# A fused macaron layer with a 64-state scan: the loop over inner batches written out, with constant waits

## What is computed

```
def step(state, inp):
    x_t, dt_t, B_t, C_t = inp
    dA = jnp.exp(dt_t[:, :, None] * A[None])
    state = state * dA + (dt_t * x_t)[:, :, None] * B_t[:, None, :]
    y_t = jnp.einsum('bds,bs->bd', state, C_t)
    return (state, y_t)
...
y = y + x_ssm * D[None, None, :]
y = y * jax.nn.silu(z)
return x + y @ Wout
```

## Time and profile before

| | us |
|---|---|
| median of 3 runs | 5524.71 |
| lowest, highest | 5524.02, 5534.78 |
| the profiled execution: time | 5548.79 |
| the profiled execution: span from first to last instruction | 5546.0 |

### The profile page before, as it was taken

How to read it: one execution, slowest core, us unless ns; L and a number is a source line. 1 busy time by engine, 2 the same in 40 slices (tenths; PEclk the granted TensorE clock), 3 DMA queues, 4 the chain that set the end, 5 groups by cost and what they waited for, 6 DMA issues and landing times.

```text
span 5546.0 us, 203591 instructions
## 1 busy us (share of the span) xinstructions
PE 4869.8 (88%) x85070; PEld 3076.2 (55%) x85070; DVE 4916.4 (89%) x4595; ACT 3918.0 (71%) x6659; POOL 5028.8 (91%) x2310
## 2 busy tenths in 40 slices
PE   4798989989899898988989899898988989899887
PEld 2455555555555555555555555555555555555554
DVE  1699999989998998989989999998989989999997
ACT  3777777767777676776767778676776767766564
POOL 0699998999989899898999989999898999999997
PEclk9899999999999999999999999999999999999999
DMA  5565655656556565565656556565565655556553
GB/s 166 151 168 196 166 185 177 176 186 162 191 168 183 180 172 186 165 186 175 171 193 165 184 179 176 192 162 193 171 182 183 170 189 170 182 184 172 190 179 123
DMA packets 579015, 977.63 MB, mean 176 GB/s; under 512 B 294881, under 2 KB 328450, under 8 KB 510466
## 3 DMA queue, kind: packets, MB, share of 16 engines
q1 hardware_dynamic: 313858, 961.82, 54.2%
q10 hardware_dynamic: 264192, 2.11, 2.8%
HBM read 875.74 MB, written 88.08 MB: 174 GB/s over the span
## 4 chain that ended last, share of the span: by engine, by line
POOL 59%; issue 25%; PE 8%; DMA 3%; DVE 2%; ACT 1%; POOLq 1%; ACTq 0%; DVEq 0%; SPq 0%
POOL H L665 56%; PE pUB L729 3%; PE Y L755 3%; DMA Cb<-scratch_c 2%; DVE H L607 2%; PE pP L686 1%; POOL lnv L641 1%; POOL dto L646 1%; PE pP L692 1%; POOL duo L652 1%; POOLq L664 0%; PE pA L775 0%; DVE cv L558 0%; PE pA L769 0%; ACT junk L193 0%
## 5 line engine op out<-in xcount | busy, mean ns | idle before, releaser
L665 POOL TENSOR_TENSOR H<-H,Cb 128x1024 f32<-128x1024 f32 x2048 | 4796.1, 2397 | 322.0 <-DVE H L607 315.3
L607 DVE TENSOR_TENSOR_SCAN H<-dA,pUB 128x512 f32<-128x512 f32 x4096 | 4675.8, 1202 | 444.0 <-PE pUB L729 417.7
L444 ACT ACTIVATE dA<-DT,w_negA 128x512 f32<-128x512 f32 x4096 | 2620.4, 711 | 1271.2 <-DVE H L607 1267.8
L729 PEld LDWEIGHTS pUB<-Bd,UT 64*64 64x64 f32 x65536 | 1961.7, 134 | 1357.7 <-issue 1339.0
L729 PE MATMUL pUB<-Bd,UT 64*64 64x128 f32 x65536 | 2267.3, 274 | 452.5 <-DVE H L607 380.0
L755 PE MATMUL Y<-H,w_ident 64*64 64x512 f32 x16384 | 2034.1, 602 | 103.8 <-POOL H L665 99.8
L755 PEld LDWEIGHTS Y<-H,w_ident 64*64 64x64 f32 x16384 | 681.6, 135 | 680.9 <-issue 664.5
L686 PE MATMUL pP<-hT,w_Win 128*128 128x512 f32 x512 | 281.1, 675 | 15.3 <-DVE cv L558 12.1
L692 PE MATMUL pP<-U,w_dt_w 128*128 128x512 f32 x512 | 257.3, 627 | 6.6 <-DVE ev L621 4.8
L444 ACT ACT_TABLE_LOAD x178 | 228.4, 1283 | 3.3
L558 DVE SCALAR_TENSOR_TENSOR cv<-pP,w_conv_w,cv 128x511 f32<-128x511 f32 (+2 forms) x192 | 139.3, 725 | 34.0 <-ACT cv L382 33.7
(11 more groups left out here) (80 smaller groups left out, 1740.4 us busy)
## 6 DMA issues: line engine op xcount, KB each, us to landing
Cb<-scratch_c SPq DMA_DIRECT2D x512, 1024.0 KB, 5.3
Bd<-scratch_diag SPq DMA_DIRECT2D x512, 512.0 KB, 4.2
scratch_diag<-H SPq DMA_DIRECT2D x16, 1024.0 KB, 18.0
scratch_z<-zo SPq DMA_DIRECT2D x64, 256.0 KB, 5.7
scratch_dt<-dto SPq DMA_DIRECT2D x64, 256.0 KB, 7.3
scratch_ut<-uto SPq DMA_DIRECT2D x64, 256.0 KB, 6.2
DT<-scratch_dt SPq DMA_DIRECT2D x64, 256.0 KB, 5.1
UT<-scratch_ut SPq DMA_DIRECT2D x64, 256.0 KB, 5.9
```

Of the source, the lines that this page charges most:

```text
L444: last = nc.scalar.activation(dA[:, n % DAR, j, :], DT[:, k, :], ACT.Exp, scale=c["negA"][:, k, GS * blk + j:GS * blk + j + 1])
L607: last = nc.vector.tensor_tensor_scan(H[:, n % HR, 2 * i + j, :], dA[:, n % DAR, 2 * i + j, :], pUB[:, i, :].rearrange("p (t s) -> p s t", ...
L665: nc.gpsimd.tensor_tensor(h[:, j:j + 2, :], h[:, j:j + 2, :], Cb[:, blk % 2, j:j + 2, :], ALU.mult).then_inc(times_c, 1)
L729: last = nc.tensor.matmul(out, UT[rows, k, j * P + h * HP:j * P + h * HP + HP], Bd[rows, blk % 2, i, j * P:(j + 1) * P].rearrange("p (t s) ...
```

## The change

The loop is written out: steps 1 to 13 are traced one after the other in Python, so there is no jump back and every count is a constant. The instruction `pe.sem_inc(pe_go, 1)` goes at its four places, so the wait (the last one, where there are several) stands at the first product. Two table entries move the fourth turn of `duo` from unit 50 to 52 on PE, its copy on ACT from 52 to 54 and its store on SP from 53 to 56. The loads of `DT` and `UT` move from units 60 and 61 to 50 and 54 (tiles 0 and 1 of the next step) and from units 4 and 5 to 10 and 14 (tiles 2 and 3).

```diff
-SPS = {"load x": (0,), "load r": (2,), "store z": (6, 10, 14, 18), "store C": (22,), "store dt": (31, 37, 43, 49),
-       "store u": (37, 43, 49, 53), "load z": (28, 29, 36, 37), "store out": (48,), "store r": (42,)}
+SPS = {"load x": (0,), "load 2": (10, 14), "load 0": (50, 54), "load r": (2,), "store z": (6, 10, 14, 18), "store C": (22,), "store dt": (31, 37, 43, 49),
+       "store u": (37, 43, 49, 56), "load z": (28, 29, 36, 37), "store out": (48,), "store r": (42,)}
...
-        "store B": (25, 26, 29, 30, 31, 32, 35, 37), "dt": (27, 33, 39, 45), "log": (28, 34, 40, 46), "turn u": (36, 42, 48, 52),
+        "store B": (25, 26, 29, 30, 31, 32, 35, 37), "dt": (27, 33, 39, 45), "log": (28, 34, 40, 46), "turn u": (36, 42, 48, 54),
...
-       "turn u": (34, 40, 46, 50), "turn 1": (13, 16), "turn c": (32, 35), "turn 3": (51, 54)}
+       "turn u": (34, 40, 46, 52), "turn 1": (13, 16), "turn c": (32, 35), "turn 3": (51, 54)}
...
         step(0, True, False, True, True)
-        with engine.Fori(1, NB - 2) as b:
+        for b in range(1, NB - 2):
             step(b, True, True, True, True)
...
-                    if scan and n in (4, 5):
-                        load_du(b, n - 2)
+                    if scan and n in when["load 2"]:
+                        load_du(b, 2 + when["load 2"].index(n))
...
-                    if proj and n in (GN - 4, GN - 3):
-                        load_du(q, n - GN + 4)
+                    if proj and n in when["load 0"]:
+                        load_du(q, when["load 0"].index(n))
...
                 pe.wait_ge(state_done, at(2 * u + i - 1))
-                pe.sem_inc(pe_go, 1)
                 for j in range(NJ):
```

More of the change, by code:

```diff
@@ L261, in layers @@
     d_in, c_in = [sem(f"d_in{i}") for i in range(2)], [sem(f"c_in{i}") for i in range(2)]
-    u_kept, pe_go, d_blank, d_st, rs_one = sem("u_kept"), sem("pe_go"), sem("d_blank"), sem("d_st"), sem("rs_one")
+    u_kept, d_blank, d_st, rs_one = sem("u_kept"), sem("d_blank"), sem("d_st"), sem("rs_one")
     decay, forced, state_done, times_c, summed, skip, gated = (sem(n) for n in ("decay", "forced", "state_done", "times_c", "summed", "skip", "gated"))
@@ L271, in ffns @@
     def ffns(b):
-        return min(b + 2, NB) if isinstance(b, int) else b + 2
+        return min(b + 2, NB)
     def steps(engine, step):
@@ L325, in step @@
                 c_, q, a = b - 1, b + 1, b + 2
[L326 to L329, removed]
+                when = SPS
                 for n in range(GN):
@@ L337, in step @@
                     if scan and n % 2 == 0 and seq < 2 * NBLK - 1:
-                        load_block(b if n < HALF else twin, seq + 1, GN * b + n)
-                    if scan and n in (4, 5):
-                        load_du(b, n - 2)
+                        load_block(b, seq + 1, GN * b + n)
+                    if scan and n in when["load 2"]:
+                        load_du(b, 2 + when["load 2"].index(n))
                     if close and n in when["load r"]:
@@ L370, in step @@
                         load_block(q, 0, GN * q - 2)
-            again = sp.alloc_register("again")
             sp.wait_ge(zero, at(1))
@@ L419, in store_diagonals @@
                 act.wait_ge(b_out, at(q + 1))
-                if isinstance(q, int) and q < 2:
+                if q < 2:
                     act.wait_ge(d_blank, at(16 * FILLS * (q + 1)))
```

## The result

The kernel after takes 5455.3 us (median of 4 runs, 5452.2 to 5459.0). The kernel before, run beside it on the same chip, takes 5529.7 us (median of 4, 5524.0 to 5537.1). The ratio is 0.985 with a 95% interval of 0.9834 to 0.9866; the two medians differ by 74.5 us, and their quotient, 0.9865, lies at the upper edge of that interval. The time lies inside the predicted range, 8 us above the predicted 5447. The profiled execution took 5459.0 us where the one before took 5548.8, and the sum made against that time had said 5459.

What follows compares the result with a forecast made beforehand. POOL, busy about 314 us a step, was taken as the bound, with only its idle time winnable. Against the profiled 5548.8 us: -87.2 -8 -2 +7, about -90, 5459; for the runs 5447 us, range 5420 to 5485.

Steps and rivals of the forecast that it cites:

- The jumps, -87.2: Loop written out: removing twelve jumps back per engine wins the surplus of steps 2 to 13 over step 1, 87.2 us.
- The direct part, 5.6 us a jump: At a jump: PE's 3.82 us pause reaches POOL as 4.5 us, about 5.6 with the slow products behind.
- The waits at the products, -8: PE's waits at products: each real wait 0.10 us shorter, five a step count, 16 scanned steps: 8 us.
- upper bound of 34: PE's waits at products: if all 21 waits of a step counted, 2.1 us a step, 34 us in all.
- The fourth turn, -2: Turn of duo near unit 51: moving it can win POOL's next gap, 0.23 us; 0 to 3.5 us, taken as 2.
- DT and UT, 0: Loads on SP: moving them gains nothing at the boundary, and Cb's slack covers the new place; 0 us.
- No Cb wait: Profile after: expected to show no wait for a Cb transfer.
- More code, 0: Instruction fetch: written-out code is read no more than before, as the looped body was fetched anew every turn; 0 us.
- Rival (c): Written-out code stalls on its own fetch, 1.57 us each; at seven a step slower, 5590 us; chance 0.04.
- Slow stretches that come back, +7: Clock at 1.2 GHz: slow stretches return in two of thirteen steps, 3.1 us each, rounded up to 7 us.
- Rival (a): Jumps go but all thirteen steps have slow-clock stretches, 3.1 us each, 40 us instead of 7; 5480 us; chance 0.13.
- two readings of the 24 us: Profiled run's 24.1 us excess: in the stalls that go, runs end at 5459 us; elsewhere, at 5435; middle taken.

Runs made afterwards that it cites:

- The first experiment: Kernel before with only the loop changed: steps 1 to 13 written out, counts constant, separate wait instructions, turns and loads unmoved; 5469.7 us, ratio 0.9875.
- the wait apart: Kernel after with the separate wait instruction put back on PE at its four places; 5475.8 us, beside 5458.3 for the kernel after on the same chip.
- the last experiment: Kernel after with first sums into X, first feed-forward's products and two norm 2 statistics moved later; 5495.5 us, beside 5460.9 for the kernel after.
- second set: Kernel after unchanged, run again beside its versions with the separate wait, turn or loads put back; 5458.3 us, ratio 0.9858 to the kernel before.
- third set: Kernel after unchanged, run on another chip beside a repeat of its version with the loads back; 5460.9 us, ratio 0.9837 to the kernel before.
- first set: Kernel after unchanged, the runs of the main result; 5455.3 us beside 5529.7 for the kernel before, ratio 0.9850.

## Why the prediction held, point by point

**The bound.** POOL is still the pace, busy for 314 us of each step. Its idle time in a plain step is 13.6 us, as "near 14" had said; step 1 of before was a good picture of what every step would become.

**The jumps, -87.2.** Right in cause, 18 us too large as a term. The loop alone brought 69 us (interval 58 to 80). The prediction took the whole surplus of steps 2 to 13 over step 1 as the jumps' and set 7 us of clock against it; the split is 68 us of jumps and 19 us of slow stretches. The first experiment kept 3959.3 - 12 x 328.4 = 18 us over step 1, of which some 7 are its two stalls and the rest its five slow steps. The direct part, 5.6 us a jump, was close: 68 / 12 = 5.7, and five jumps in place of twelve follow it. What the step left out is that the sum has two engines in it: with PE's jump gone, DVE's 1.03 us comes to the surface. One row was misread: of the 13 waits of PE for "issue" in steps 2 to 13 of before, ten are at jumps and not twelve. The pauses at the jumps into steps 10 and 11, 3.02 and 3.12 us, stand under DVE's name, and the three others are 0.25, 0.80 and 1.57 us inside steps.

**The waits at the products, -8.** The latency was right, and what it is worth was not. Over the waits for the scan in steps 2 to 13, `force` starts 0.05 us behind it in the median in after, and 0.15 us behind it with the wait apart. The scan ahead of a waiting `force` in after:

```profile
1915.05 1.21 DVE L603 TENSOR_TENSOR_SCAN H<-dA,pUB 128x512 f32<-128x512 f32 x1
...
1916.31 1.10 PE L724 MATMUL pUB<-Bd,UT 64*64 64x128 f32 x32 [0.16 <-DVE H L603]
```

It ends at 1916.26 and the product starts at 1916.31, 0.05 us later, where it was 0.15. It reaches POOL at four places a step before unit 51, not five, for 0.3 us and not 0.5, and the undisturbed step is no shorter for it (327.7 us with and without). Yet the whole edit brought 14 to 17 us, by fewer stalls of straight code and, in these runs, fewer slow steps. Neither had a term, and neither is shown to follow from the shorter wait. The prediction's upper bound of 34 held the amount, but by luck: it had been worked out from the latency alone.

**The fourth turn, -2.** Nothing. The gap of 0.23 us that it was to remove is gone in plain steps with the turn at either place.

**DT and UT, 0.** Right. POOL waited for one Cb of step 0 in after, 1.6 us, and for one in the same step of before, 1.9 us. In the later steps of each profiled run at most one Cb was late: by 0.6 us in three of the six runs with the loads at the new place, and by 0.3 to 1.6 us in five of the eight at the old.

```profile
POOL H L661 <- DMA Cb<-scratch_c: 1.6, 1, 1.6
```

"No Cb wait" was thus not quite what was seen, and the row of before had been there to read.

**More code, 0.** Right, and a little better: the instruction queues of after carry less than the earlier trace rows.

```profile
q8 instruction: 668, 10.94, 0.8%
q14 instruction: 142, 1.16, 0.1%
```

Together 12.1 MB against 13.7. Rival (c), stalls of straight code, stayed rare but was larger where it came than its price of 1.57 us: 3.6 and 4.9 us in the first experiment, 3.9 and 3.9 in the kernel with the wait apart, and none that the waits list for `force` over steps 2 to 13 of the kernel after. Step 0 of after has two, 1.33 and 1.23 us. The change got by with so few because the waits stand at the products, or by chance; that isn't shown.

**Slow stretches that come back, +7.** Right in size for the kernel after. Its six profiled runs (three as it is, three with the turn or the loads back) have 18 slow steps among 72, each 3.0 us longer than a plain one: 12 x 0.25 x 3.0 = 9 us. Rival (a), all steps slow, is what the last experiment became by another edit: 331.2 us a step, 35 us lost where (a) had put 33. So it was a real rival.

**From the profile to the runs.** The sum against the profiled time, -90, came out as 89.8. It held because errors cancelled. In the spans, the loop alone goes from 5546.0 to 5472.2, that is 73.8 less where the sum had -87.2 + 7 = -80; the other three edits go on to 5457.0, that is 15.2 less where it had -10. The prediction had two readings of the 24 us by which that run lay over the others, and took the middle. The first was the better: in after the profiled run lies 4 us over its median, and the time is 5455 and not 5435. So the excess probably sat in what went; no trace of a shorter run of before is there to show it.

## What stays open

Two steps of one run can be alike to the hundredth of a microsecond and still part at the clock. In the kernel after (second set), step 3 and then step 6, PE:

```profile
1254.52 1.10 PE L724 MATMUL pUB<-Bd,UT 64*64 64x128 f32 x32 [1.86 <-DVE H L603]
1255.55 3.32 PE L682 MATMUL pP<-hT,w_Win 128*128 128x512 f32 x4
...
2240.69 1.10 PE L724 MATMUL pUB<-Bd,UT 64*64 64x128 f32 x32 [1.86 <-DVE H L603]
2241.72 1.98 PE L682 MATMUL pP<-hT,w_Win 128*128 128x512 f32 x4
```

Both come 81 us after POOL's first product of their step, behind the same wait of 1.86 us. The same four products take 3.32 us in one and 1.98 in the other, and the granted clock of the 4 us around them is 0.57 and 1.00:

```profile
1255.50:1259.50 4.00, 4.00 (x26) 1.67 (x24) 3.31 (x3) 3.42 (x8) 4.00 (x3) 0.57 0.13 49
2241.70:2245.70 4.00, 4.00 (x52) 2.06 (x52) 4.00 (x4) 3.41 (x8) 3.88 (x3) 1.00 0.31 114
```

The work ahead of them doesn't tell them apart, nor does the DMA rate of 49 against 114 GB/s, since the other plain steps of this run have 49 to 64 at the same place. What differs is when the step begins, seen against the clock record. Within one run, the instants at which the granted clock changes all fall on evenly spaced marks. Measured against these, the two slow steps of this run (3 and 13) begin later than all ten plain ones, by 0.02 us at the least, and step 3 by 0.27 us later than step 6. In the runs with the turn back and with the loads back (both sets) the slow steps begin later than the plain ones, too. In the third set of the kernel after one plain step doesn't fit, and in the first set the two kinds overlap. Steps 3 to 13 of the last experiment, all slow, begin 0.2 to 0.4 us later than step 13 here. This is read from the records; no run moved a step on purpose.

The stretch costs POOL 1.1 us at unit 16, 1.6 more in units 17 to 34, and 3.0 us by the end of the step. Why an edit behind that place (the last experiment) brings it in every step isn't settled. Nor is what makes straight code stall 188 us into some steps. The wait at the product within the looped kernel wasn't tried.

## What to carry to other kernels

Compare the steps that are entered by a jump with the one that isn't: their difference, and the wait on each engine's first instruction behind the jump, price the loop before anything is changed. Price each engine's jump, since the longer hides the shorter, and split the surplus into the pause itself and the slow-clock stretches, for only the first is sure to go. Where a difference between two versions is no more than a few of those stretches or a stall or two, repeat both on another occasion before believing it.

## What was not expected of the hardware

- A jump back over one step's code (some 10600 products and weight loads on PE) costs PE 3.0 to 4.4 us and DVE 0.9 to 1.1 us before their first instruction, and 5.7 us of each step's 334; a hint ahead of it cuts PE's pause to 0.9 to 1.5 us at seven boundaries and to 1.8 to 2.5 at the other five.
- A separate wait instruction costs 0.10 us of latency at a wait (0.15 against 0.05 us), and an undisturbed step is no longer for it (327.7 us).
- Straight code on PE can stall for 3.6 to 4.9 us with nothing waited for: twice in steps 2 to 13 of two written-out kernels each, 188 us into the step every time.
- The same kernel in two sets of runs, on two chips, gave 5465.7 to 5472.3 and 5453.6 to 5458.6 us, without overlap.
